# The last two stores of a streaming kernel leave as 120 rows and 8 rows each

## The reference

```python
w = weights[subjects]
out = jnp.einsum('bct,bcd->bdt', x, w)
return x + out
```

## Time and profile before

| what | value |
|---|---|
| median of three runs | 326.37 us |
| lowest and highest | 325.66 and 327.25 us |
| the profiled execution's own time | 326.79 us |
| its span, first to last instruction | 324.8 us |
| granted TensorE clock over the span, share of full | 0.972 |
| PE, VectorE, ScalarE, GpSimd busy | 74%, 49%, 40%, 16% of the span |
| bytes moved by DMA | 134.78 MB, mean 415 GB/s |
| loads, median from issue to landing | 35.0 us for 1024 KB |
| stores, median from issue to landing | 35.5 us for 1024 KB |

### The profile page before, as it was taken

How to read it: one execution, slowest core, us unless ns; L and a number is a source line. 1 busy time by engine, 2 the same in 40 slices (tenths; PEclk the granted TensorE clock), 3 DMA queues, 4 the chain that set the end, 5 groups by cost and what they waited for, 6 DMA issues and landing times.

```text
span 324.8 us, 4203 instructions
## 1 busy us (share of the span) xinstructions
PE 239.8 (74%) x1032; PEld 111.6 (34%) x1032; DVE 160.2 (49%) x130; ACT 130.0 (40%) x129; POOL 52.7 (16%) x137
## 2 busy tenths in 40 slices
PE   3499999999787787786776867768768677687600
PEld 1145555554243343342332332323323333333200
DVE  0437767767546446355354464453544645535410
ACT  1026646556434334334244243342443433424400
POOL 2132122222111111111111011111110111100000
PEclk9979999999999999999999999999999999999955
DMA  7999999999999999999999999999999999999992
GB/s 267 423 422 423 425 427 427 426 426 428 427 428 428 427 427 428 427 428 425 430 424 430 424 428 427 428 427 427 427 428 426 429 426 427 428 426 428 427 428 123
DMA packets 19478, 134.78 MB, mean 415 GB/s; under 512 B 2066, under 2 KB 3091, under 8 KB 3091
## 3 DMA queue, kind: packets, MB, share of 16 engines
q1 hardware_dynamic: 10256, 67.64, 49.7%
q10 hardware_dynamic: 9218, 67.11, 49.0%
HBM read 67.63 MB, written 67.11 MB: 415 GB/s over the span
## 4 chain that ended last, share of the span: by engine, by line
PE 73%; DVE 11%; ACT 5%; issue 2%; DMA 1%; DVEq 1%; POOL 1%; POOLq 1%; ACTq 0%
PE products L140 72%; DVE out_ring L168 10%; ACT out_ring L189 5%; DMA loaded<-weights 1%; DVE table L153 1%; PE products L123 1%; DVEq L37 1%; POOL selected L112 1%; POOLq L107 0%; POOLq L112 0%; ACTq L187 0%; POOLq L101 0%; DVEq L173 0%; POOLq L111 0%; DVEq L152 0%
## 5 line engine op out<-in xcount | busy, mean ns | idle before, releaser
L140 PE MATMUL products<-x_ring,selected 64*128 64x512 f32 x1024 | 234.2, 601 | 61.9 <-DVE out_ring L168 35.0
L168 DVE COPY out_ring<-products 64x1024 f32<-64x1024 f32 x128 | 156.4, 1222 | 140.2 <-PE products L140 138.2
L189 ACT COPY out_ring<-products 64x1024 f32<-64x1024 f32 x128 | 128.7, 1006 | 177.6 <-PE products L140 176.1
L140 PEld LDWEIGHTS products<-x_ring,selected 64*128 64x128 f32 x1024 | 109.3, 188 | 186.7 <-issue 139.3
L112 POOL COPY selected<-table 64x256 f32 x128 | 51.0, 398 | 234.8 <-PE products L140 177.9
L123 PE MATMUL products<-loaded,spread 128*128 128x512 f32 x8 | 5.7, 876 | 5.4 <-DMA loaded<-weights 5.4
L153 DVE TENSOR_TENSOR table<-products,unit 128x1024 f32<-128x1024 f32 x2 | 3.8, 1942 | 9.2 <-PE products L123 9.2
L123 PEld LDWEIGHTS products<-loaded,spread 128*128 128x128 f32 x8 | 2.2, 295 | 8.0 <-issue 8.0
L189 ACT ACT_TABLE_LOAD x1 | 1.3, 1283 | 1.5 <-PEq L210 1.5
L96 POOL TENSOR_SCALAR_AFFINE_SELECT unit<-ones 64x256 f32<-64x256 f32 x2 | 0.8, 404 | 0.1
L88 POOL TENSOR_SCALAR_AFFINE_SELECT spread<-ones 128x256 f32<-128x256 f32 x1 | 0.4, 419 | 0.1
## 6 DMA issues: line engine op xcount, KB each, us to landing
x_ring<-x SPq DMA_DIRECT2D x64, 1024.0 KB, 35.0
out<-out_ring ACTq DMA_DIRECT2D x64, 1024.0 KB, 35.5
loaded<-weights SPq DMA_DIRECT2D x1, 512.0 KB, 4.3
subject_row<-subjects ACTq DMA_DIRECT2D x1, 0.5 KB
```

What stands on the lines that cost most here:

```text
L140: last = nc.tensor.matmul(products[:, b, g, n * BANK:(n + 1) * BANK], selected[part, k, e * mixed:(e + 1) * mixed], x_ring[part, s, e * ti ...
L168: nc.vector.tensor_copy(out_ring[0:HALF, s, b * times:(b + 1) * times], products[b * HALF:(b + 1) * HALF, s % PSUM_BUFS, 0, :]).then_inc(e ...
L189: nc.scalar.copy(out_ring[HALF:channels, s, b * times:(b + 1) * times], products[b * HALF:(b + 1) * HALF, s % PSUM_BUFS, 1, :]).then_inc(o ...
```

## The change

ScalarE's last turn is taken out of the loop and written out with constants. In it, the stores of the last two places (tiles 62 and 63) are two DMAs each: rows 0 to 119 and rows 120 to 127. Each of the two adds 16 to the place's semaphore, and the last waits expect 16 more for these two places.

```diff
+SPLIT_TILES = 2
+PARTS = [(0, 120), (120, 128)]
...
-            def go_round(turn, first=False):
+            def go_round(turn, first=False, last=False):
...
-                    act.dma_start(out_rows[bass.ds(tile * channels, channels), :],
-                                  out_ring[:, s]).then_inc(stored[s], DMA)
+                    for a, b in PARTS if last and s >= TILES_PER_TURN - SPLIT_TILES else [(0, channels)]:
+                        act.dma_start(out_rows[bass.ds(tile * channels + a, b - a), :],
+                                      out_ring[a:b, s]).then_inc(stored[s], DMA)
 
             go_round(0, first=True)
-            with act.Fori(1, turns) as turn:
+            with act.Fori(1, turns - 1) as turn:
                 go_round(turn)
+            go_round(turns - 1, last=True)
             for s in range(TILES_PER_TURN):
-                act.wait_ge(stored[s], turns * DMA)
+                extra = len(PARTS) - 1 if s >= TILES_PER_TURN - SPLIT_TILES else 0
+                act.wait_ge(stored[s], (turns + extra) * DMA)
```

## The result

The changed kernel takes 331.18 us (median of four, 330.49 to 331.81) against 326.71 us before (median of four, 325.66 to 327.25). The ratio is 1.014, with a 95% interval of 1.0104 to 1.0177: 4.5 us more, where 2.8 us less was forecast.

What follows compares the result with a forecast made beforehand. It took the 16 DMA engines as the bound, the slowest working alone at the end. Relieving it gave 3.4 us, two extra rows took 0.6, other terms 0: 326.37 - 2.8 = 323.6 us, range 322.6 to 327.1.

Steps and rivals of the forecast that it cites:

- The kernel is bound by the DMA engines, and one engine sets the end.: Whole kernel: a 128 MB stream through 16 full DMA engines; at the end one works alone for 3.4 us.
- 120 rows on 15 engines, 8 on 8.: Split stores of tiles 62 and 63: 8 rows per engine on 15 engines, then 1 row each on 8.
- Rival 2: Split stores run on fewer engines, such as 120 rows on eight: slower, 327.9 or 331.3 us; chance 0.09.
- The slowest engine is the one left out: Tiles 62 and 63: the slowest engine gets 0 rows instead of 16, saving 4.9 us on it; chance 0.66.
- rival 1: Tiles 62 and 63: the slowest engine isn't left out; 326.4 us, or 327.0 with 18 rows; chance 0.22.
- A row takes 0.306 us whatever the shape of its DMA.: Last stores: a row of 8192 bytes costs its engine 0.306 us, also in the split DMAs.
- the second engine's two rows: Tiles 62 and 63: two extra rows on the second-slowest engine cost 0.6 us, moving its end from 320.9 to 321.5.
- The added issues are hidden.: ScalarE's two extra store issues, 0.34 us each, cost 0, covered by idle time and some 6 us of queued rows.
- The straight code costs nothing.: Last turn written out: cost 0, with an instruction fetch of 1.05 us kept as the far end.

Runs made afterwards that it cites:

- The searches: Three variants of the changed kernel: tile 62 stored whole, tile 63 as 112 rows plus four small DMAs with own semaphores; 329.63, 326.90 and 328.58 us, one execution each.
- Halves: Changed kernel with the last two stores split into 64 and 64 rows instead of 120 and 8; ratio 1.0103 against the kernel before.
- the bench: Separate kernel with transfers alone, no computing, four tiles' DMAs per stage: stores of 128 rows 11.4 us, 120 rows 14.8; loads 12.3 and 21.1.

## Why the prediction was wrong, step by step

- *The kernel is bound by the DMA engines, and one engine sets the end.* Right: in each profiled execution of the kernel and its variants one engine works alone at the end.
- *120 rows on 15 engines, 8 on 8.* Right (25 increments). Rival 2 gave 331.3 us for a split over eight engines, near the measured 331.2, but by a mechanism that didn't happen; that it is near is luck.
- *The slowest engine is the one left out* (0.66, named as the weak point). This failed. It is number 4, and its 18 rows instead of 16 cost 0.6 us, as rival 1 has it. The argument, that a peculiar engine stands at an end of the list, was a guess. The Trainium skill's page "DMA: Bandwidth & Descriptors", section "Latency and other measured facts", names DMA engines 7 and 15 as the usually slower ones. The searches don't bear that out for this kernel: the slowest was number 4. All stores in the trace of before run on all 16 engines and couldn't tell; it took DMAs on fewer, as in the searches.
- *A row takes 0.306 us whatever the shape of its DMA.* This failed too, and it is the larger part. With rival 1's rows alone the time would have been 327.0 us; it was 331.2. I bounded the row's price for the second engine's two rows and for nothing else, so the range had no place for it. What stands in its place: the fast engines land tile 61 from 315.0 us on and go over to the split tiles while the slowest one is still at whole stores, and from then on its rows last longer. That is the 0.5 us of tile 60 and the 2.7 us of tile 61, stores that the change doesn't touch. Halves (no engine with more rows, 3.4 us slower) and the split along the row (no change) frame it from both sides. That they meet on the slowest one's partitions is inferred from the bench; which engine reads which partition in the kernel, no trace shows.
- *Even a relieved engine would not have brought 2.8 us.* The bench gives 0.11 us more for a row of a 120-row store (3.4 us / 32), which is 1.7 us for the 16 rows of each engine. Also, the slowest engine would have been held up all the same: its last whole store, tile 61, landed at 322.75, only 1.5 us before the end of the kernel before. Both are estimates and not run, since no DMA here could be kept from the first engines of the list.
- *The added issues are hidden.* Right, though one of 8 rows took 0.86 and 0.94 us, not 0.34:

```profile
305.15 1.25 ACTq L199 DMA_DIRECT2D out<-out_ring  x2
307.54 2.03 ACT L192 COPY out_ring<-products 64x1024 f32<-64x1024 f32 x2 [2.91 <-PE products L143]
310.10 1.30 ACTq L199 DMA_DIRECT2D out<-out_ring  x2
```

  The first two are over at 306.4, before the copies at 307.5, and the last at 311.4, when the engines have rows until after 315.
- *The straight code costs nothing.* Right (ratio 0.9996).

What stays open: why engine 4 falls behind, why the clock stayed low until 21 us in some executions, and how much of the 4.5 us goes with that. No version that beats both kernels was run. Number 4 could be avoided by DMAs of at most four rows, but four neighbouring rows lie as close as each four of the eight in the bench, whose rows took 1.25 us.

## What to carry to other kernels

Where DMA is the bound, count in bytes what each engine still has to do at the end, but don't relieve an engine before its number is known: a few small DMAs at the end of the kernel, of different numbers of rows and with semaphores of their own, can show it in one execution. Keep all 128 partitions in large DMAs, above all in those that compete with others. A split along the row (two times 4096 bytes here) cost nothing; splits across partitions made rows last up to two times as long, four times with eight neighbouring ones, and slowed stores that the change hadn't touched. A transfer's price measured in one shape is no price for another.

## What the runs showed of the hardware

- Loads into 120 partitions, issued alone, run at 209 GB/s, loads into 128 at 427 (bench, one execution).
- A row of 8192 bytes took an engine 0.31 us alone, 0.64 us beside one 32 partitions away (101 GB/s at 0.49 of 16 engines' time), and 1.25 us with four engines on four neighbouring partitions.
- A DMA of 120 rows sets 15 of its 16 increments only with its data; one of n rows under 16 has n + 1 increment events, the first of them at the issue.
- Issuing a DMA of 1 to 8 rows beside full queues took 0.28 to 1.02 us, one of 128 rows 0.34.
- The slowest DMA engine was number 4 (counted as in the searches) in the one execution that shows it from both sides, and in none of the three searches was it the last in the list. In the kernel before, a store's last increment came 1.4 us behind its eighth one in tile 16, 3.0 in tile 32 and 5.2 in tile 56: the lag grows along the stream.
